# Attention with 8-bit weights: value products four heads behind the exponentials instead of five, and a fourth buffer for the exponentials' bytes

## The reference

```python
q = _fq_sym(q, axis=-1)
k = _fq_sym(k, axis=-1)
v = _fq_sym(v, axis=2)
attn = jnp.einsum('bhqd,bhkd->bhqk', q, k)
attn = jax.nn.softmax(attn.astype(jnp.float32), axis=-1)
attn = _fq_unsigned(attn, axis=-1)      # 8 bits, the largest weight of a row is 255
out = jnp.einsum('bhqk,bhkd->bhqd', attn, v)
```

## Time and profile before

| | |
|---|---|
| runs | 1324.37 us median, 1318.36 to 1325.68 |
| profiled execution | 1332.7 us, span 1331.0 us, mean granted TensorE clock 0.953 |
| the exponentials (L995) | from 123.8 to 792.1 us of the span |
| instructions | 24350 |

### The profile page before, as it was taken

One profiled execution on the slowest core, in us unless ns is written; L12 is line 12 of the kernel. 1 busy time (PEld: TensorE's weight loads), 2 busy tenths in 40 slices (PEclk: granted clock), 3 DMA queues, 4 the chain that ended last, 5 costly groups with the idle time before them and its releaser, 6 DMA issues. The chain is left out here.

```text
span 1331.0 us, 24350 instructions
## 1 busy us (share of the span) xinstructions
PE 1097.1 (82%) x8392; PEld 647.3 (49%) x8507; DVE 956.5 (72%) x1705; ACT 890.3 (67%) x1519; POOL 767.6 (58%) x648
## 2 busy tenths in 40 slices
PE   5967888888888888888788898869999946999992
PEld 4643344444444444444444465435666634657771
DVE  5988999889999999999989968422223399642333
ACT  4556899898999999999899985321334267423440
POOL 3220777777778787888767874664245200443662
PEclk9998999999999999999999999889999976999996
DMA  9901777878778676676666659201398640114667
GB/s 307 323 0 24 149 157 156 174 146 157 158 162 182 147 149 108 115 119 107 97 103 112 112 89 272 80 24 40 75 261 194 182 131 5 62 66 82 105 105 215
DMA packets 379120, 174.70 MB, mean 131 GB/s; under 512 B 297419, under 2 KB 370795, under 8 KB 379000
## 3 DMA queue, kind: packets, MB, share of 16 engines
q1 hardware_dynamic: 363064, 154.39, 51.7%
q0 software_dynamic: 14832, 17.70, 7.8%
q10 hardware_dynamic: 1104, 1.05, 0.2%
HBM read 48.71 MB, written 57.71 MB: 80 GB/s over the span
## 5 line engine op out<-in xcount | busy, mean ns | idle before, releaser
L995 ACT ACTIVATE weight<-bank,bias,sq_all 128x1024 uint8<-128x1024 f32 x512 | 610.2, 1201 | 52.4 <-issue 24.9
L963 DVE TENSOR_REDUCE top<-bank 128x1 f32<-128x512 f32 (+1 forms) x683 | 612.2, 951 | 43.9 <-PE bank L811 34.1
L1043 POOL CAST weight<-turned 128x2048 bf16<-128x2048 uint8 x256 | 482.8, 1892 | 124.1 <-PE bank L845 109.6
L829 PE MATMUL bank<-kT,query 128*128 128x512 bf16 x916 | 287.6, 386 | 57.1 <-ACT weight L995 42.6
L845 PEld LDWEIGHTS bank<-v_sb,weight 128*128 128x128 bf16 x4096 | 173.1, 97 | 105.1 <-issue 3.5
L811 PE MATMUL bank<-kT,qT_all 64*128 64x512 bf16 x683 | 135.6, 392 | 54.6 <-DVE top L963 54.6
L845 PE MATMUL bank<-v_sb,weight 128*128 128x16 bf16 x4096 | 173.1, 170 | 0.9 <-POOL weight L1043 0.3
L811 PE MATMUL bank<-kT,query 128*128 128x512 bf16 x334 | 128.7, 385 | 3.2 <-DVE top L963 2.6
L829 PEld LDWEIGHTS bank<-kT,query 128*128 128x128 bf16 x1024 | 60.1, 97 | 139.1 <-ACT weight L995 97.3
L2239 POOL DMA_INDIRECT dispatched_rows<-rows,put x32 | 34.4, 1076 | 117.8 <-ACT rows L2211 84.0
L995 ACT ACTIVATION_READ_ACCUMULATOR weight<-bank,bias,sq_all 128x1 f32 x512 | 101.8, 199 | 0.0
(11 more groups left out here) (310 smaller groups left out, 1559.0 us busy)
## 6 DMA issues: line engine op xcount, KB each, us to landing
dispatched_rows<-zeros SPq DMA_DIRECT2D x42, 530.0 KB, 3.5
expert_sums<-zeros SPq DMA_DIRECT2D x20, 512.0 KB, 6.0
rows<-dispatched_rows SPq DMA_DIRECT2D x71, 132.5 KB
attn<-expert_sums SPq DMA_DIRECT2D x12, 512.0 KB, 5.3
attn<-in_L_ffn_w_down SPq DMA_DIRECT2D x32, 176.0 KB
wgu<-in_L_ffn_w_gate SPq DMA_DIRECT2D x24, 176.0 KB
wgu<-in_L_ffn_w_up SPq DMA_DIRECT2D x24, 176.0 KB
query<-qT_all SPq DMA_DIRECT2D x32, 128.0 KB, 3.2
```

The costliest lines, as they stand in the source:

```text
L829: mm = pe.matmul(unit[u % 2][:, v * 512:(v + 1) * 512], query2[:, t % 2, h, :], kT[:, h // 2, first + v * 512:first + (v + 1) * 512], star ...
L963: ve.tensor_reduce(top[:, first:first + count], bank[:, first % 3:first % 3 + count, :], AX.X, ALU.max).then_inc(s_max, 1)
L995: ac.activation(weight8[:, n % 3, u * 1024:(u + 1) * 1024], unit[u], ACT.Exp, bias=bias[:, n:n + 1], scale=sq_all[:, n:n + 1], accum_out=n ...
L1043: po.tensor_copy(weight[:, n % 3, :, :, :].rearrange("p c q two -> p (c q two)"), turned8[:, n % 3, :, :].rearrange("p c q -> p (c q)").bi ...
```

## The change

`BEHIND` goes from 5 to 4, `weight8` gets a fourth buffer, and the exponentials of head n wait for the transpose of head n-4 in place of n-3. `turned8` and `weight` keep three buffers, and their two waits stay.

```diff
-            weight8 = sa("weight8", [P, 3, NTOK], U8)
+            weight8 = sa("weight8", [P, 4, NTOK], U8)
...
-            LEAD, BEHIND = 6 * NBLOCK, 5
+            LEAD, BEHIND = 6 * NBLOCK, 4
...
-                    if n >= 3:
-                        ac.wait_ge(s_turn[n % 3], 16 * (n // 3))
+                    if n >= 4:
+                        ac.wait_ge(s_turn[(n - 4) % 3], 16 * ((n - 4) // 3 + 1))
...
-                        ac.activation(weight8[:, n % 3, u * 1024:(u + 1) * 1024], unit[u], ACT.Exp, bias=bias[:, n:n + 1],
+                        ac.activation(weight8[:, n % 4, u * 1024:(u + 1) * 1024], unit[u], ACT.Exp, bias=bias[:, n:n + 1],
...
-                    sp.dma_start_transpose(turned8[:, n % 3, :, :], weight8[:, n % 3, :].bitcast(U16)).then_inc(s_turn[n % 3], 16)
+                    sp.dma_start_transpose(turned8[:, n % 3, :, :], weight8[:, n % 4, :].bitcast(U16)).then_inc(s_turn[n % 3], 16)
```

## The result

The changed kernel takes 1279.31 us (median of four runs, 1276.91 to 1281.34) against 1324.19 us (four runs of before, 1318.36 to 1325.68). The ratio is 0.9673, with a 95% interval of 0.9646 to 0.9699: 44.9 us faster. The forecast was 1291 us with 1281 to 1306.

A forecast was written before the change was run, and what follows sets the result against it. Attention was taken to be held by a ring through the buffers whose late transposes stall ACT. Stalls of 32.6 us plus 0.6 us at the end gave 33.2 us: 1324.4 - 33.2 = 1291 us, range 1281 to 1306.

The forecast's parts named there:

- The ring, and what ends it: Attention: value products, widening, transpose, exponential, each three heads apart; earlier products and a fourth buffer set ACT's landing stalls to zero.
- The example, head 202, cured by the distance alone: ACT idled 1.72 us before this exponential; with value products one head earlier its transpose would land at 648.7, before 649.7.
- The length of the attention, 32.6 us: ACT's waits of 24.9 + 5.5 us and 2.18 us at 151.03 all vanish and shorten the tiles in full.
- my own count of landings: ACT's idle times over 0.1 us ending 0.07 to 0.08 us after head n-3's transpose landed: 46, making 33.8 us.
- The case of all DVE's idle time: Rival, chance 0.05: all DVE idle time goes, 42 us with outer tiles and the end, giving 1282 us.
- The end of the stage, 0.6 us: End of attention: the last cast no longer waits for value products and starts earlier, 0.6 us won.
- Those 8.3 us I leave outside: The profiled execution, 1332.7 us, lay 8.3 us above the median; the gain was subtracted from 1324.4 us instead.
- The other side, knife's edge at heads 4k+3: POOL casts behind biases awaiting DVE's maximum: 0.11 us room at head 79, 18 heads under 0.3, PE waits next to nothing.
- SP waits for the widening in few heads: Profile sign on SP's queue: waits for the widening in few heads in place of 214.
- POOL's waits: Profile sign: waits for value products fall from 109.6 us to under 30; those for landings and the group maximum grow.
- Tile ends on DVE at nothing: DVE's tile ends at L948 and L952 move three blocks earlier; no wait shows there now, so they gain nothing.
- The rule for a late wait: Between transpose and value products: by the skill's rule, taking a head out exposes DMA latency and the time goes up.

## Why the prediction was right in kind and short in size

- *The ring, and what ends it*: right. Both parts alone end it (634.1 and 636.2 us), and with both, no wait for a landing is left and every inner tile takes 39.4 to 39.5 us, where 39.6 was forecast.
- *The example, head 202, cured by the distance alone*: not tried on the same landings. With the distance alone head 202 is not among the 12 waits that are left, and by number 34 of 46 such stalls go.
- *The length of the attention, 32.6 us*: too small. It got 35.2 us shorter than in the profile that the sum was made from, and 38.0 us shorter than the mean of five profiles (671.0 - 633.0). **The price of the stalls is the first term that was off**, in three ways. I took 32.6 us from the labels of the view, where my own count of landings gave 33.8. The profile that I worked from had the shortest attention of the five (668.3, the others 670.6 to 672.6) and the least of such stalls: 33.8 us, 34.4 to 36.8 in the others, 35.1 in the mean. I took the gain from it as if it were typical. And I took ACT's own work as fixed. Its instructions cover 620.5 us of the attention now and covered 622.3 before (623.0 in the mean of five). Mostly that is overlap: an exponential that has not waited starts before the row ahead of it has ended, which 412 of them do now and 398 did. So the 35.2 us are 33.4 of ACT's idle time (46.0 - 12.6) and 1.8 of its covered time, and the 38.0 us are 35.4 and 2.6. The case of all DVE's idle time (42 us, 1282) lies near in number, but it is not what happened: 10.1 us of it are left in the inner tiles (552.36 - 542.26).
- *The end of the stage, 0.6 us*: not found. The last cast ended 5.7 us behind the last exponential in all five profiles of before, and 5.2, 5.0, 6.0 and 6.1 us behind it in the four of the changed kernel. The last outputs leave PSUM (L952) 7.9 us behind it in all five, and 7.9, 7.9, 8.5 and 8.7 us in the four. The last two casts no longer wait for value products, as worked out, but they wait for a landing instead, 2.18 us in the first profile:

```profile
757.09 3.76 POOL L1043 CAST weight<-turned 128x2048 bf16<-128x2048 uint8 x2 [2.18 <-DMA turned<-weight]
```

- *"Those 8.3 us I leave outside"*: right as arithmetic, but it let the other stages stand still with no allowance. **This is the second step that failed.** The first profile of before had 14 to 17 us more in the stage behind the attention than the three whose spans are 1321 to 1322 us (147.6 against 130.7 to 133.7), and those, not the first, stand for the median. Against their means (front 123.3, attention 671.4, stage 132.6, rest 394.6) the three of the changed kernel with spans of 1275 to 1279 us (122.4, 633.0, 129.0, 392.7) are shorter by 0.9, 38.4, 3.6 and 1.9 us, 44.8 of the 44.9. The forecast missed 11.7 us (44.9 - 33.2). Of these 5.8 us lie in the attention (38.4 - 32.6) and 5.8 us outside it (0.9 + 3.6 + 1.9, less the 0.6 forecast there). The 3.6 us of the stage behind go with its granted clock, 0.92 to 0.95 in those three of before and 0.95 to 0.97 in the changed kernel's. Whether what lies outside the attention is an effect of the change or scatter stays open: two medians of the same kernel differed by 4.4 us.
- *The other side, knife's edge at heads 4k+3*: right to 0.01 us at head 79, and PE waits once, 0.3 us, at a head 4k+3. A distance of three falls over this very edge, and the order of the biases is shown to be its larger part.
- *SP waits for the widening in few heads*: wrong. 176 heads and 129.1 us are left of 214 and 229.1, though the longest is 1.9 in place of 4.0 us. It has hardly a price, as the run with the buffer alone shows: 207 such waits, and an attention only 1.1 us longer than with both parts.
- *POOL's waits*: right, 15.8 us for value products (under 30 was forecast), 81.1 us for DVE's maximum, which had been 27.7 over the same window, and 17.1 us for landings, which had been 10.2.
- *Tile ends on DVE at nothing*: nothing in the waits speaks against it.
- *The rule for a late wait*: the Trainium skill (DMA: Bandwidth & Descriptors, Rules for kernel authors) says to wait for a DMA's semaphore late, so that its fixed cost is hidden. The trace at a distance of four does not bear out that less distance costs time: PE waits once, 0.3 us, and the time fell. The traces at a distance of three agree with it, even with the biases out of the way: PE 21.0 us and POOL 114.1 us of waiting.

## What to carry to other kernels

Where two engines are each 93% busy and tiles of the same work differ by 3 us in length, look for a ring of buffers: find one stall, follow it back through each "wait for n-3", and count the ring's slack. Here one more buffer at one link, or one step less of distance, ended it, and doing both added little. Buffers at the other two links were not tried. Before shortening a distance, list what stands ahead of each consumer on its own queue (here two tiny bias instructions ahead of every fourth cast), since that sets how far one can go: the same distance of three was 4.3% slower or 1% faster by that order alone. And take the base of a sum from several profiles: the one used here had up to 17 us too much in an untouched stage and was up to 4 us too short in the changed one.

## What the runs showed that I had not expected

Four profiles of the changed kernel have an attention of 632.8 to 633.1 us, within 0.3 us, while the kernel before scatters over 4.3 us (668.3 to 672.6). With the ring's slack used up, late landings became time (46 waits, 33.8 us, in the first profile). With slack ACT waits for none, though landings still take up to 5.8 us.

In the stage behind the attention, PE stands still with no event in the trace, in both kernels, by an amount that differs from one execution to the next. The worst case was the profiled execution of the run with the biases behind the cast, the longest of its four (1323.82 us), where that stage took 170.4 us. Ten microseconds of it in the windows view, and the matmuls in the timeline:

```profile
868.00:878.00 10.00, 2.33 (x4) 1.15 (x4) 0.00 (x0) 0.00 (x0) 7.42 (x10) 0.50 0.05 10
```

```profile
868.51 0.58 PE L1270 MATMUL bank<-swd,hT 64*128 64x256 f32 x1 [2.22 <-issue]
871.30 0.58 PE L1270 MATMUL bank<-swd,hT 128*128 128x256 f32 x1 [2.22 <-issue]
```

Here a matmul starts 2.8 us after the one before, with 2.2 us of nothing between, at a granted clock of 0.50 (1.2 GHz), while only POOL works (its scattering DMAs, L1697). What PE waits for there was not tried and stays open. The stage was up to 42.6 us longer by it than at its best (170.4 - 127.8), lower clock included.
